# A decoder of two layers on one core: a prologue in another order, chunked loads, linear attention with a denominator per token and head

## The reference

```python
q, k, v = jnp.split(x @ W_qkv, 3, axis=-1)
q = relu(split_heads(rmsnorm(q, qn_w)))      # 16 heads of 8
k = relu(split_heads(rmsnorm(k, kn_w)))
kv = jnp.einsum('bhnd,bhne->bhde', k, v)
out = jnp.einsum('bhnd,bhde->bhne', q, kv)
normalizer = jnp.einsum('bhnd,bhd->bhn', q, k.sum(axis=2)) + EPS_DEN
out = out / normalizer[..., None]
return merge_heads(out) @ W_out + b_out
```

## Time and profile before

| what | us |
|---|---|
| median of the runs | 1718.22 |
| the profiled execution | 1719.86 |
| its span, first to last instruction | 1718.1 |
| busy: PE, DVE, ACT, POOL | 1515.6, 1291.8, 1118.5, 431.6 |
| start of the maxima of the first pair | 88.8 |
| start and end of the cross attention | 156, 1050 |

### The profile page before, as it was taken

One profiled execution on the slowest core, in us unless ns is written; L12 is line 12 of the kernel. 1 busy time (PEld: TensorE's weight loads), 2 busy tenths in 40 slices (PEclk: granted clock), 3 DMA queues, 4 the chain that ended last, 5 costly groups with the idle time before them and its releaser, 6 DMA issues.

```text
span 1718.1 us, 26018 instructions
## 1 busy us (share of the span) xinstructions
PE 1515.6 (88%) x8851; PEld 543.2 (32%) x8864; DVE 1291.8 (75%) x2214; ACT 1118.5 (65%) x1496; POOL 431.6 (25%) x413
## 2 busy tenths in 40 slices
PE   2877999999999999999999997899996779978963
PEld 1512333333333333333332333343333512312312
DVE  4697878788778778887789898666665676778775
ACT  3687887666876767877767786655554367746533
POOL 5400543233443434434400010344440000000000
PEclk7866999999999999999999997999998859986986
DMA  4000000000000000000010000111100000000000
GB/s 127 7 0 6 1 1 1 2 1 7 1 1 1 1 1 3 2 1 10 20 32 1 1 1 25 31 43 41 46 23 0 1 1 1 1 0 1 1 13 12
DMA packets 12557, 20.26 MB, mean 12 GB/s; under 512 B 1671, under 2 KB 11255, under 8 KB 12343
## 3 DMA queue, kind: packets, MB, share of 16 engines
q1 hardware_dynamic: 12438, 18.76, 4.0%
HBM read 18.23 MB, written 0.52 MB: 11 GB/s over the span
## 4 chain that ended last, share of the span: by engine, by line
PE 65%; DVE 13%; issue 13%; POOL 4%; ACT 3%; DMA 1%; POOLq 0%; SPq 0%; ACTq 0%; DVEq 0%
PE PS L1752 26%; PE PS L1737 18%; PE PS L1784 5%; POOL WRK L602 4%; DVE KNB L1081 4%; PE PS L1700 3%; PE PS L1627 2%; PE PS L1619 2%; DVE WRK L1131 1%; DMA KNB<-in_ctx_fm_dram 1%; DVE QS L1137 1%; PE PS L2028 1%; PE PS L2013 1%; ACT KNB L761 1%; PE PS L1722 1%
## 5 line engine op out<-in xcount | busy, mean ns | idle before, releaser
L1131 DVE TENSOR_TENSOR WRK<-WRK 128x768 f32<-128x768 f32 (+1 forms) x500 | 552.1, 1104 | 57.1 <-ACT WRK L741 45.2
L741 ACT ACTIVATE WRK<-PS 128x1024 f32<-128x1024 f32 (+1 forms) x510 | 500.2, 1023 | 104.5 <-PE PS L1737 91.1
L1752 PE MATMUL PS<-WRK,V 128*64 128x512 f32 (+1 forms) x2040 | 496.3, 606 | 0.0
L1081 DVE CUSTOM_DVE_ANT_0 KNB<-PS,KNB 128x512 f16<-128x512 f32 (+2 forms) x464 | 331.3, 731 | 138.4 <-PE PS L1784 126.2
L575 POOL TENSOR_TENSOR WRK<-WRK 128x256 f32<-128x256 f32 x300 | 275.6, 919 | 402.4 <-ACT WRK L741 383.8
L761 ACT ACTIVATE KNB<-PS 128x512 f16<-128x512 f32 (+2 forms) x306 | 180.7, 591 | 98.1 <-PE PS L1784 98.0
L1924 PE MATMUL PS<-WRK,KNB 128*128 128x512 f16 x828 | 198.1, 384 | 11.0 <-POOL WRK L602 4.3
L1752 PEld LDWEIGHTS PS<-WRK,V 128*64 128x64 f32 (+1 forms) x2040 | 124.1, 136 | 245.6 <-issue 198.1
L1737 PE MATMUL PS<-Q,KB 64*128 64x512 f16 (+1 forms) x1428 | 192.7, 379 | 0.5 <-ACT WRK L741 0.4
L1737 PE MATMUL PS<-KNB,KB 64*128 64x512 f16 (+1 forms) x1224 | 156.5, 378 | 0.0
L602 POOL TENSOR_TENSOR WRK<-KB,WRK 128x1024 f16<-128x1024 f32 x46 | 98.6, 2143 | 134.0 <-ACT WRK L887 134.0
(11 more groups left out here) (333 smaller groups left out, 1500.5 us busy)
## 6 DMA issues: line engine op xcount, KB each, us to landing
V<-in_moe_w_dram SPq DMA_DIRECT2D x44, 192.0 KB, 2.4
KNB<-in_ctx_fm_dram SPq DMA_DIRECT2D x1, 2401.5 KB, 18.0
CTX<-in_ctx_fm_dram SPq DMA_DIRECT2D x6, 384.0 KB, 4.4
BW<-in_bit_w_dram SPq DMA_DIRECT2D x1, 960.0 KB, 5.5
PWK<-in_pair_w_dram SPq DMA_DIRECT2D x4, 192.0 KB, 2.8
SM<-in_small_dram SPq DMA_DIRECT2D x1, 716.5 KB, 4.4
XT<-in_x_fm_dram SPq DMA_DIRECT2D x1, 512.0 KB, 5.2
X<-in_x_tm_dram SPq DMA_DIRECT2D x1, 512.0 KB, 8.0
```

The costliest lines, as they stand in the source:

```text
L741: e.activation(PR[0:r, u % 2, b, :], bank(2 * b, 2 * b + 2, slice(0, r)), ACT.Exp).then_inc(S("exp"), 1)
L1081: return e.tensor_tensor_reduce(diffs, sums, diffs, 0.5, NEG, ALU.add, ALU.max, accum_out=out)
L1131: e.tensor_tensor(total, total, part, ALU.add).then_inc(S("acc"), 1)
L1752: ins = e.matmul(PS[h * HD:(h + 1) * HD, 4, :], v(r, j, h), PR[0:r, unit_no(hf, i) % 2, b, h * HALF:(h + 1) * HALF], start=(j == 0), stop= ...
```

## The change

Nine things are changed.

1. Loads: the part of `SM` that holds qk_w, w_out and w_qkv comes first (384 KB), then XT, the context in seven chunks with a semaphore each, PWK, then x by token and the rest of `SM`.
2. POOL's constants: those that others wait for come first; two tables come behind the context work.
3. The context's differences 0 and 1 and remainders 0 to 2 are made by DVE, the others by POOL, chunk by chunk; ACT copies chunk by chunk as they land.
4. Linear attention: the denominators are made by token and head (the sum of k on all partitions by a product with ones, times q, summed in eights, reciprocal of 128 columns) and go into q. The masked K^T V is multiplied by w_out once; then one set of eight products gives the projected output.
5. Key differences use banks 0 and 1, 14 of the 26 stand ahead of the LayerNorm's transposes; values use banks 3 to 5, and DVE evicts them.
6. The context's largest value leaves the prologue. In slots 9 to 21 of pair 1 SP loads chunks of 96x512 again into one buffer (`XC`), each when DVE has reduced the one before; POOL's reduction across partitions follows behind unit 24 of half 2.
7. The bitnet weight steps move to slots 7 to 21 of pair 0, and their reduction to behind unit 11 of half 0.
8. The LayerNorm of the prologue takes its small operands from PSUM.
9. `keep_busy(count, bank)`: products of 512 columns whose results nobody reads, at nine places behind the attention, 184 in all.

```diff
-BIT_AT = {34: ("sum", 0, 3), 35: ("sum", 3, 5), 36: ("sum", 5, 6), 37: ("sum", 6, 7), 40: ("scale",), 41: ("low", 0, 5),
+BIT_AT = {7: ("sum", 0, 3), 8: ("sum", 3, 5), 9: ("sum", 5, 6), 10: ("sum", 6, 7), 13: ("scale",), 14: ("low", 0, 5),
...
+DVE_DIFF, DVE_LO = 2, 3
+
+MAG_AT = {9 + c: c for c in range(NKP)}
+MAG_DONE = 9 + NKP + 1
+
+K16_EARLY, V_EARLY = 14, 6
...
-            q.dma_start(SM[:, :], small).then_inc(S("ld_small"), 16)
+            q.dma_start(SM[:, FIRST_SMALL:NSMALL], small[:, FIRST_SMALL:NSMALL]).then_inc(S("ld_x"), 16)
             q.dma_start(XT[:, :], x_fm).then_inc(S("ld_x"), 16)
-            q.dma_start(X_[:, :, :], x_tm.rearrange("(t p) d -> p t d", p=P)).then_inc(S("ld_x"), 16)
-            q.dma_start(CTX32, ctx_fm).then_inc(S("ld_ctx"), 16)
+            for c, (a, w) in enumerate(KCH):
+                q.dma_start(CTX32[:, a:a + w], ctx_fm[:, a:a + w]).then_inc(S(f"ld_ctx{c}"), 16)
             q.dma_start(PWK[:, :, :], pair_w[0, :, 0:3, :]).then_inc(S("ld_pwk"), 16)
+            q.dma_start(X_[:, :, :], x_tm.rearrange("(t p) d -> p t d", p=P)).then_inc(S("ld_small"), 16)
+            q.dma_start(SM[:, 0:FIRST_SMALL], small[:, 0:FIRST_SMALL]).then_inc(S("ld_small"), 16)
...
+                if p == 1:
+                    q.wait_ge(S("a0_dve"), 6)
+                    for c, (a, w) in enumerate(KP):
+                        if c:
+                            q.wait_ge(S("axp"), c)
+                        q.dma_start(XC[:, 0:w], ctx_fm[:, a:a + w]).then_inc(S("ld_cx"), 16)
...
+            def difference(c):
+
+                a, w = KCH[c]
                 w = min(w, NC - LAG - a)
+                for k in range(c, min(c + 2, NKC)):
+                    e.wait_ge(S(f"ld_ctx{k}"), 16)
                 e.tensor_tensor(D32[:, a:a + w], CTX32[:, LAG + a:LAG + a + w], CTX32[:, a:a + w],
                                 ALU.subtract).then_inc(S("d32"), 1)
-            e.wait_ge(S("c_hi"), 1)
-            for a, w in KCH:
-                ins = e.tensor_tensor(C_LO[0:DC, a:a + w], CTX32[:, a:a + w], C_HI[0:DC, a:a + w], ALU.subtract)
-            link(ins)
-            e.sem_inc(S("c_lo"), 1)
-            e.wait_ge(S("d_hi"), 1)
+
+            def remainder(c):
+
+                a, w = KCH[c]
+                e.wait_ge(S("c_hi"), c + 1)
+                e.tensor_tensor(C_LO[0:DC, a:a + w], CTX32[:, a:a + w], C_HI[0:DC, a:a + w],
+                                ALU.subtract).then_inc(S("c_lo"), 1)
+
+            difference(2)
+            difference(3)
+            remainder(3)
+            for c in range(4, NKC):
+                difference(c)
+            for c in range(4, NKC):
+                remainder(c)
+            e.wait_ge(S("ctx_dve"), DVE_DIFF + 1)
...
-            e.wait_ge(S("ax"), 1)
-            e.partition_all_reduce(AM[:, 0:1], AX[:, 0:1], P, RED.max).then_inc(S("am"), 1)
...
-                    if hf == 1 and i == 12:
+                    if hf == 2 and i == MAG_DONE + 1:
+                        e.wait_ge(S("ax"), 1)
+                        e.partition_all_reduce(AM[:, 0:1], AX[:, 0:1], P, RED.max).then_inc(S("am"), 1)
+                    if hf == 0 and i == 11:
...
             e.wait_ge(S("ld_x"), 32)
-            link(e.tensor_tensor(R[:, :, :], X_[:, :, :], over_tiles(sm("b_out")), ALU.add))
-            for c, (a, w) in enumerate(KCH):
-                ins = e.tensor_reduce(AXP[0:DC, c:c + 1], CTX32[:, a:a + w], X, ALU.max, apply_absolute_value=True)
-            ins.then_inc(S("axp"), 1)
-            e.tensor_reduce(AX[0:DC, 0:1], AXP[0:DC, :], X, ALU.max).then_inc(S("ax"), 1)
+            qk_w = sm("qk_w").rearrange("p (a d) -> p a d", a=2)
+            for t in range(NT):
+                e.wait_ge(S("v0"), t + 1)
+                ins = e.tensor_tensor(QK0[:, :, t, :], PS[:, t, 0:2 * D].rearrange("p (a d) -> p a d", a=2), qk_w, ALU.mult)
+                if t in (1, 4):
+                    difference(t // 3)
+            link(ins)
             e.tensor_scalar(RMS.rearrange("p (t a) -> p t a", a=2), SS, 1.0 / D, RMS_EPS, ALU.mult,
                             ALU.add).then_inc(S("a0_dve"), 1)
+            e.wait_ge(S("a0_act"), 1)
             link(e.reciprocal(RMR, RMD))
-            for t in range(NT):
-                for a in range(2):
-                    ins = e.scalar_tensor_tensor(QK0[:, t, a, :], PS[:, t, a * D:(a + 1) * D],
-                                                 RMR[:, 2 * t + a:2 * t + a + 1], w[:, a * D:(a + 1) * D],
-                                                 ALU.mult, ALU.mult)
+            rms = RMR.rearrange("p (t a) -> p t a", a=2)
+            for a in (1, 0):
+                ins = e.scalar_tensor_tensor(QK0[:, a, :, :], QK0[:, a, :, :], 0.0,
+                                             rms[:, :, a].unsqueeze(2).to_broadcast([P, NT, D]), ALU.max, ALU.mult)
+                if a:
+                    ins.then_inc(S("a0_dve"), 1)
             link(ins)
             e.wait_ge(S("a0_pe"), 1)
-            link(e.tensor_tensor(KVB[:, 0:D], KVS[:, 0:D], MASK, ALU.mult))
-            e.tensor_scalar(KVB[:, D:2 * D], MASK, KVS[:, D:D + 1], None, ALU.mult).then_inc(S("a0_dve"), 1)
-            link(e.tensor_scalar(DEN, bank(5, 7), DEN_EPS, None, ALU.add))
-            link(e.reciprocal(QS2, DEN))
-            e.tensor_tensor(ON[:, :], bank(3, 5), QS2, ALU.mult).then_inc(S("a0_dve"), 1)
+            link(e.tensor_tensor(QKS.rearrange("p (t d) -> p t d", t=NT), QK0[:, 0, :, :], over_tiles(PS[:, 0, 0:D]),
+                                 ALU.mult))
+            link(e.tensor_reduce(DEN0[0], QKS.rearrange("p (n d) -> p n d", d=L0D), X, ALU.add))
+            link(e.tensor_scalar(DEN0[1], DEN0[0], DEN_EPS, None, ALU.add))
+            link(e.reciprocal(DEN0[2], DEN0[1]))
+            for h in range(2):
+                part = QK0[:, 0, 4 * h:4 * h + 4, :].rearrange("p t (n d) -> p (t n) d", d=L0D)
+                n_ = 4 * L0H
+                e.tensor_tensor(part, part, DEN0[2][:, h * n_:(h + 1) * n_].unsqueeze(2).to_broadcast([P, n_, L0D]),
+                                ALU.mult).then_inc(S("a0_dve"), 1)
+            e.wait_ge(S("a0_pe"), 2)
+            e.wait_ge(S("consts"), 2)
+            e.tensor_tensor(VK0, PS[:, 1, 0:D], MASK, ALU.mult).then_inc(S("a0_dve"), 1)
+            for c in range(DVE_LO):
+                a, w = KCH[c]
+                e.wait_ge(S("c_hi"), c + 1)
+                split_lo(C_LO[0:DC, a:a + w], CTX32[:, a:a + w], C_HI[0:DC, a:a + w]).then_inc(S("ctx_dve"), 1)
             k_weights(0)
             v_weights(0)
-            link(e.tensor_tensor(r2, bank(1, 3), r2, ALU.add))
-            ln(1)
-            link(e.tensor_tensor(R[:, :, :], X_[:, :, :], over_tiles(sm("bo")), ALU.add))
+            e.wait_ge(S("ld_small"), 32)
+            link(e.tensor_tensor(R[:, :, :], X_[:, :, :], over_tiles(sm("b_out")), ALU.add))
+            e.wait_ge(S("a0_pe"), 6)
+            link(e.tensor_tensor(r2, bank(6, 8), r2, ALU.add))
+            ln_beside_pool()
+            for g in range(V_EARLY):
+                first_values(g, 3 + g % 3)
             q_out(0, 0, 2)
             q_out(0, 1, 7)
+            for g in range(V_EARLY, NVG):
+                first_values(g, 3 + g % 3)
+            e.tensor_tensor(R[:, :, :], X_[:, :, :], over_tiles(sm("bo")), ALU.add).then_inc(S("a0_dve"), 1)
             for c in range(NKP):
-                k_out(0, c, 3 + (NVG + c) % 4)
+                k_out(0, c, 3 + (NVG + c) % 3)
...
+                    if p == 1 and s in MAG_AT:
+                        c = MAG_AT[s]
+                        e.wait_ge(S("ld_cx"), 16 * (c + 1))
+                        e.tensor_reduce(AXC[0:DC, c:c + 1], XC[:, 0:KP[c][1]], X, ALU.max,
+                                        apply_absolute_value=True).then_inc(S("axp"), 1)
+                    if p == 1 and s == MAG_DONE:
+                        e.wait_ge(S("axp"), NKP)
+                        e.tensor_reduce(AX[0:DC, 0:1], AXC[0:DC, :], X, ALU.max).then_inc(S("ax"), 1)
...
+            def keep_busy(count, b):
+
+                for _ in range(count):
+                    e.matmul(bank(b), ones_b[:, :], BQ[:, 512:512 + HALF], start=True, stop=True)
...
             for t in range(NT):
-                ins = e.matmul(PS[:, 0, 0:D + 1], QK0[:, t, 1, :], VA[:, t, :], start=(t == 0), stop=(t == NT - 1))
+                ins = e.matmul(PS[:, 0, 0:D], ones[:, :], QK0[:, 1, t, :], start=(t == 0), stop=(t == NT - 1))
             ins.then_inc(S("a0_pe"), 1)
             for t in range(NT):
-                ins = e.transpose(PS[:, 1 + t // 4, (t % 4) * P:(t % 4 + 1) * P], QK0[:, t, 0, :], ident[:, :])
+                ins = e.matmul(PS[:, 1, 0:D], VA[:, t, :], QK0[:, 1, t, :], start=(t == 0), stop=(t == NT - 1))
             ins.then_inc(S("a0_pe"), 1)
-            e.wait_ge(S("a0_dve"), 3)
-            e.wait_ge(S("q0_fm"), 1)
-            for a in range(2):
-                for h in range(2):
```

(43 more changed lines are left out.)

210 lines of the change are left out of this document (119 added, 91 removed).

## The result

The changed kernel takes 1702.94 us (median of four, 1697.55 to 1704.93) against 1718.91 of the kernel before (four, 1718.14 to 1719.77): ratio 0.9915, 95% interval 0.9897 to 0.9934. I had 1710.5 and 1698 to 1721, "faster" at 0.74. In later comparisons the kernel before lay between 1711.58 and 1720.05; the changed one, in the one in which it ran again, between 1698.13 and 1703.55, and its ratio there was 0.9912 (0.9896 to 0.9927).

The account below looks back on a forecast made before the run. Bounds: a mostly DVE chain of waits until 88.7 us, PE from 154 to 1050, then often half clock. Terms −11.5 + 8 + 1.5 + 1 + 1 − 7.5 = −7.5 gave 1710.5 us against a 1718.2 median; range 1698 to 1721.

Parts of the forecast that it names:

- Prologue: Everything up to the first product of the maxima: at 77.3 instead of 88.8, −11.5 us (bounds −23 to −4).
- The start: Start of the prologue: with smaller loads first, the QKV products begin at 5.8 us instead of 9.87.
- K is ready at 15.9: Prologue, linear attention: DVE's first 1024-column operation takes 1.27 and K is ready at 15.9 us, before at 35.72.
- The 8.7 for the six turns: Prologue: 8.7 us added because six DVE operations with two SBUF operands take turns with POOL, ending at 38.8.
- ACT had only 6 of 26 key-side evictions: Prologue: 12 of 26 key evictions remain behind Q, with seven value groups between, 1.66 per pair, ending at 66.6 us.
- my own sign of being wrong: Prologue: the forecast is wrong if the maxima begin before 70 or after 84 us.
- Bit steps: Bitnet weight steps and reduction moved into half 0: +1.5 for a longer POOL wait, +1 for DVE's steps.
- Abs-max reduction: POOL's reduction across partitions behind half 2: 5.8 us of waiting and about 2 of half clock, +8 (6 to 11).
- Abs-max in pair 1: DVE's thirteen reductions of reloaded context chunks in pair 1 fit, but not in every slot: +1 us (0 to +16).
- rival 3: Pair 1: the thirteen loads land too slowly and delay DVE, 15 us, giving 1725.5 us; chance 0.12.
- Fill: 184 filling matmuls behind the attention keep PE's clock up: −7.5 us (−3 to −9).
- Rival 1: Prologue: DVE hardly waits for POOL, so the prologue ends at 69 and the time is 1702.5 us; chance 0.20.

Follow-up runs that it names:

- the third experiment: The changed kernel with the 16 reciprocals of the root mean squares in PSUM instead of SBUF: 1700.26 us.
- experiment 1: The changed kernel run again with no edit: 1701.53 us, ratio 0.9912 to the kernel before.
- experiment 5: The kernel before with only the bitnet steps moved to slots 7 to 21 of pair 0 and their reduction to half 0: 1715.98 us, ratio 1.0002.
- experiment 9: The changed kernel with reciprocals in PSUM, abs-max reduction behind half 5, fill of 10 dropped, bitnet sums in the prologue, their reduction beside the maxima: 1685.13 us.
- experiment 4: The changed kernel with POOL's reduction of the context's largest value moved from half 2 to behind the last add of half 5: 1693.68 us.
- experiment 6: The changed kernel with the context's remainders 0 to 2 made by POOL instead of DVE: 1699.71 us, ratio 0.9911.

## Why the prediction came out as it did

The direction was right and the time lay in the range, 7.6 above the measured one: 7.5 us faster was forecast, 16 were measured. The abs-max reduction and the fill had the right mechanism, the prologue had the right one in part and a wrong count, and the bitnet term had the wrong sign. By the profiled spans, −22.3 stands against the −7.5 of the sum (the fill's terms as they are listed add to −7.8, and 1718.2 less 7.5 is 1710.7); term by term:

- **Prologue: −16.9 instead of −11.5.** The start was right (5.89 for 5.8). "The first operation of 1024 columns 1.27: K is ready at 15.9" failed in the first profile: 3.36, ready at 19.93, because of the wait for POOL which I had read in the earlier trace rows and priced at nothing for these two, though a sentence beside it said that it could be so. What the Trainium skill states in "SBUF — State Buffer", section "Who interferes with whom", the third experiment shows here: with one operand moved to PSUM and nothing else, 6.64 became 2.35. The row that I gave as a sign of it is a weak one, though: the 2.04 at 42.00 is a `TENSOR_SCALAR` (L1063), with one tensor and one column of scalars; the 2.08 before it (L1062) is the one with two tensors in SBUF. The 8.7 for the six turns was too much by about as much as K came late: the six took 10.1, 5.0 of it waiting, and the statistics began at 40.57, against 40.05 forecast. In experiment 1's profile it was the other way round, K ready at 16.43 and 7.5 us of waiting in the six, and the statistics at 39.29: what DVE does not wait in one place it waits in the next. The failing step is "ACT had only 6 of 26 key-side evictions … the other 12 evictions run with seven value groups between, 1.66 per pair, → 66.6". There are 14, not 26: I counted two per 512 columns where the kernel does two per 1024, which ACT's L654 rows in the profile of before would have told (26 of them in the kernel before, and 14 of 26 in the change, are the same miscount):

```profile
57.84 1.26 ACT L654 ACTIVATE KNB<-PS 128x512 f16<-128x512 f32 x3 [0.20 <-PE PS L1612]
59.31 0.28 ACT L654 ACTIVATE KNB<-PS 128x130 f16<-128x130 f32 x1 [0.21 <-PE PS L1612]
```

  These two rows end a run that has five more of x2 ahead: 14. All 14 stand ahead of Q, and from Q's end at 57.5 (56.5 forecast) only the seven value groups followed, until 61.65: 4.1 us where I had 10.1. These 6.0 us are more than the 5.4 by which the maxima began earlier than forecast (71.87 for 77.3). That the 40.05 came true was luck, as two errors of 4 us cancelled. By my own sign of being wrong, maxima before 70, one of the four profiles of this prologue (69.92) is just outside.
- **Bit steps: −4.2 in the profiles, −2.0 by the marks and 0.0 by the median of experiment 5, instead of +2.5.** The waiting was right in kind: POOL was away for 13.6 us (14.5 forecast), and the exp then waited 4.22, below the 5 to 6 that I had named:

```profile
194.16 0.49 POOL L617 PARTITION_ALL_REDUCE BT<-BR  x1 [6.01 <-issue]
201.69 8.79 POOL L606 TENSOR_TENSOR WRK<-WRK 128x256 f32<-128x256 f32 x8 [7.05 <-issue]
...
202.52 1.94 ACT L795 ACTIVATE WRK<-PS 128x1024 f32<-128x1024 f32 x2 [4.22 <-POOL WRK L606]
```

  The step that failed is the balance of the two halves: I added the work of 11 us at +1 in half 0 and did not take away what it cost in half 1, whose whole loss of 9.0 came back. How much of the 9.0 was the reduction (I had put about 7) and how much the steps is not shown. In half 0 the steps cost more than my +1: those that stayed there in experiment 9 cost 2.6. And the wait of 6.3 was reckoned from a later unit than the one the change names (the add at 218.32 stands three units behind it). Whether half clock follows is the spread.
- **Abs-max reduction: +5.4 instead of +8.** Predicted 5.8 of wait, and these rows have 5.55. I added 2 for the half clock behind it; the clock did fall (0.58 from 496 to 500 us), yet the whole half lost 5.4, and 5.7 by experiment 4, hardly more than the wait:

```profile
489.14 0.38 POOL L614 PARTITION_ALL_REDUCE AM<-AX  x1 [5.79 <-issue]
496.53 0.71 POOL L606 TENSOR_TENSOR WRK<-WRK 4x256 f32<-4x256 f32 x1 [7.01 <-issue]
...
497.36 1.94 ACT L795 ACTIVATE WRK<-PS 128x1024 f32<-128x1024 f32 x2 [5.55 <-POOL WRK L606]
```

- **Abs-max in pair 1: 0 instead of +1.** DVE's thirteen reductions began in their slots without a wait for a load; rival 3, at +15 us, did not come. It asked for a landing above 3.1; it was 2.4, as the row of this size had.
- **Fill: −6.2, of which 5.8 to 6.1 are shown to be the fill's, instead of −7.5.** Rows halved where I said so: 3.78 became 1.98, 2.08 became 1.16, 3.59 became 2.05. The group ahead of the mixture of experts brought 1.14 (−1.2 forecast), the ten cost 0.99 (+1.0), the groups ahead of the bitnet stage brought 2.84 (−2.9). What the sum lacked is the 1.0 lost within the bitnet attention; and the 22 and 16 brought 0.15 instead of 0.6.

Rival 1 had the time (1702.5) by luck: DVE did wait for POOL, the prologue was 71.9 and not its 69, and the rest came from other terms. That the medians are 16 apart and the profiles 22 is in part the clock behind the reduction of half 0, 2.2 to 4.5 us where it falls, and a kernel before that differs by 3.9 us in its own prologue between two profiles (88.80, and 84.93 in experiment 5, whose prologue has the same code).

## What to carry to other kernels

Count a loop's iterations from the rows of the profile (its x and the number of its pieces) before multiplying: a wrong count moved this forecast by 6 us, more than any doubtful duration. When a DVE operation with its operands in SBUF waits for POOL, moving its small operand to PSUM takes the wait out of it (6.64 to 2.35), but look behind it: here most of the gain went into the next wait, and when DVE was 9.2 us earlier (experiment 6) ACT's queue took it all. A reduction across partitions on POOL kept it from its adds for 13.0 to 14.5 us wherever it stood between them, so it belongs where POOL has nothing to do before and after: that alone was worth 5.7 us in the profile, a third of what the whole change gained.

## What was not expected of the hardware

- The same wait in the same place let the granted clock fall to 0.5 in six profiles and not in three, and where it fell it was for 3.4 or 6.8 us: a spread of 4.8 us in half 0 that no instruction explains. The same happened at the end of the mixture of experts, where the clock held in one profile alone (experiment 4).
- POOL's first `affine_select` waited 11.85 us, from 2.5 to 14.3, in the changed kernel, where it stands behind only constants; it sets the start of POOL's context work (16.5), although the chunks for POOL's first difference had landed by 11.8. No run tried to avoid it.
- The same program gave prologues of 69.92 and 71.87 us, by who comes first at POOL's and DVE's turns (experiment 3). The same prologue code also gave 84.93 and 88.80: there a turn is 1.8 of it, and the granted clock much of the rest, as products stood at 1.06 us in one profile and 0.59 in the other.
